# A decoder layer with a spiking delta-rule recurrence: sign weights made earlier, norm roots spread by transposes, two steps of the vector engine's round reordered

## The reference

```python
# 1: a gated delta-rule recurrence, 8 heads, key width 64, value width 128, 512 steps
h = silu(causal_conv4(rms(layernorm(x)) * w_norm_in))
q, k, v = h@wq, h@wk, h@wv              # q and k divided by their norms
step:  mem = 0.9*mem + sd;  hard = mem > 0.5;  mem -= 0.5*spike
       alpha = sigmoid(ab + alpha_spike*spike);  beta = sigmoid(bb + sum(spike*beta_spike))
       s = s*alpha;  s = s - beta*k (k.s) + beta*k v;  out = s.q
y = z + (rms(out)*w_hn) @ w_out * gate(z);  y = y + silu(h2@w_ff1)*(h2@w_ff3) @ w_ff2
x = x + y
# 2: cross attention to 77 context rows, 16 heads, then a layernorm
x = x + layernorm(attention(layernorm(x), ctx) @ Wo + bo + residual)
# 3: three dense layers whose weights are +1 or -1, from boolean arrays
h = [l, -l], l = layernorm(x)
x = x + s2*(2*relu(s1*(2*relu(s0*(h @ sign(k0))) @ sign(k1))) @ sign(k2))
```

## Time and profile before

| | us |
|---|---|
| median of 3 runs | 1086.62 (1082.25 to 1088.74) |
| the profiled execution: its time | 1083.42 |
| its span | 1081.7 |
| PE busy | 964.8 (89%) |
| DVE busy | 680.3 (63%) |
| ACT busy | 503.6 (47%) |
| POOL busy | 208.5 (19%) |

### The profile page before, as it was taken

How to read it: one execution, slowest core, us unless ns; L and a number is a source line. 1 busy time by engine, 2 the same in 40 slices (tenths; PEclk the granted TensorE clock), 3 DMA queues, 4 the chain that set the end, 5 groups by cost and what they waited for, 6 DMA issues and landing times. The chain is left out here.

```text
span 1081.7 us, 40059 instructions
## 1 busy us (share of the span) xinstructions
PE 964.8 (89%) x16722; PEld 643.0 (59%) x16722; DVE 680.3 (63%) x2386; ACT 503.6 (47%) x1506; POOL 208.5 (19%) x394
## 2 busy tenths in 40 slices
PE   7888768999999998999999888889899999999997
PEld 2332246777777777777777776556446446446542
DVE  2887887888888888888767664236335424624710
ACT  7677313555555565555565554413224323423411
POOL 7100200212212122122121220221201210310300
PEclk9999958999999999999999998979999999999999
DMA  3000000000000000000001004000000000000100
GB/s 98 0 1 1 1 2 3 4 4 5 4 5 4 4 5 4 4 5 4 4 4 30 4 5 127 12 10 22 2 1 27 18 1 19 24 1 4 31 0 10
DMA packets 18652, 13.83 MB, mean 13 GB/s; under 512 B 2491, under 2 KB 17259, under 8 KB 18475
## 3 DMA queue, kind: packets, MB, share of 16 engines
q1 hardware_dynamic: 18475, 11.28, 3.7%
HBM read 7.70 MB, written 1.05 MB: 8 GB/s over the span
## 5 line engine op out<-in xcount | busy, mean ns | idle before, releaser
L1087 PE MATMUL banks<-work 64*64 64x64 f32 x3072 | 98.7, 234 | 16.0 <-DVE gates L775 5.9
L1148 PE MATMUL banks<-work 64*64 64x32 f32 x2560 | 106.7, 223 | 6.5 <-ACT work L1550 5.2
L203 DVE SCALAR_TENSOR_TENSOR mom<-gates 128x16 f32<-128x16 f32 x512 | 104.1, 203 | 8.8
L1480 ACT COPY work<-banks 128x128 f32<-128x128 f32 x160 | 43.0, 269 | 136.9 <-PE banks L1123 136.6
L199 DVE SCALAR_TENSOR_TENSOR gates<-mom,gates 128x16 f32<-128x16 f32 x512 | 98.0, 191 | 9.5 <-ACT gates L1453 4.5
L1148 PEld LDWEIGHTS banks<-work 64*64 64x64 f32 x2560 | 91.4, 137 | 18.7 <-issue 10.5
L775 DVE COPY_PREDICATED gates<-work,banks 128x256 f32<-128x256 uint32 x192 | 101.7, 529 | 1.1
L780 DVE TENSOR_TENSOR work<-work,banks 128x128 f32<-128x128 f32 x160 | 45.9, 287 | 83.8 <-PE banks L1148 81.8
L1087 PEld LDWEIGHTS banks<-work 64*64 64x64 f32 x3072 | 73.3, 138 | 34.0 <-issue 23.4
L669 POOL TENSOR_TENSOR mom<-mom 128x4 f32<-128x4 f32 x32 | 6.6, 207 | 387.5 <-ACT work L1529 387.5
L746 DVE TENSOR_TENSOR work<-work 128x256 f32<-128x256 f32 x160 | 68.0, 425 | 17.3 <-PE banks L1087 13.8
(11 more groups left out here) (276 smaller groups left out, 2155.3 us busy)
## 6 DMA issues: line engine op xcount, KB each, us to landing
work<-gates SPq DMA_DIRECT2D x28, 38.5 KB
qT<-in_x_dram SPq DMA_DIRECT2D x4, 256.0 KB, 3.8
work<-in_x_dram SPq DMA_DIRECT2D x4, 256.0 KB, 2.7
out_dram<-work SPq DMA_DIRECT2D x4, 256.0 KB, 2.3
gates<-in_w_ff_dram SPq DMA_DIRECT2D x3, 256.0 KB, 3.1
wv_sb<-in_wv_dram SPq DMA_DIRECT2D x1, 512.0 KB, 5.0
work<-in_w_out_dram SPq DMA_DIRECT2D x1, 512.0 KB, 4.1
gates<-in_x_Wq_dram SPq DMA_DIRECT2D x1, 512.0 KB, 5.3
```

Of the source, the lines that this page charges most:

```text
L203: ve.scalar_tensor_tensor(neg_mem, mem[:, :, t], 1.0, mem[:, :, t], ALU.is_gt, ALU.subtract)\
L1087: last = pe.matmul(level_out(l)[to, a], KS[rows, n.two, hp], late[rows, hp], start=True, stop=True)
L1148: last = pe.matmul(packed(psXT, l)[rows, a], Z[rows, l - 1, z], second_half(XT[:, n.two], l)[rows, a], start=True, stop=True)
L1480: ac.copy(first_half(Z[:, l - 1], l), z_out(l)).then_inc(z_ok, 1)
```

## The change

1. POOL makes the sign weights in the recurrence's pass i = 30 (`prev.it == ROUNDS - 3`), between `root(29)` and `root(30)`, and not at the tail's start; the two small scalings (L1718, L1719) go behind the tail's first root.
2. `spread_root` uses a PE transpose of the broadcast roots where it used a matmul with the identity. The result is the same.
3. PE's `turn_out(prev)` goes from the end of step 3 to step 4, behind `make_z(nxt, 4)`.
4. DVE, step 4: two scan operations stand together ahead of `prefix`, where one was ahead of it and one between `prefix` and `suffix`. Step 5: `prefix`, `suffix` and `keep` follow each other, and four scan operations come behind `keep`, where two of them stood between and one ahead. Steps 1 to 3 are as before.

```diff
                 def body(prev, cur, nxt, aft, aft2, gate, gate_old, scan, ramp):
                     if prev:
                         root(prev)
+                    if prev and prev.it == ROUNDS - 3:
+                        sign_weights()      # the five lines that the tail's start loses, with their waits
                     if aft2:
                         keys(aft2)
...
                         if l == 4 and gate:
                             drive(gate)
-                        spike(scan, h + (4 if l == 4 else 2))
+                        if l < 4:
+                            spike(scan, h + 2)
+                        if l == 4:
+                            spike(scan, h + 4)
+                            spike(scan, h + 5)
                         if aft:
                             prefix(aft, l)
-                        spike(scan, h + (5 if l == 4 else 3))
+                        if l < 4:
+                            spike(scan, h + 3)
                         if aft:
                             suffix(aft, l)
-                        if l != 4:
+                        if l < 4:
                             spike(scan, h + 4)
                         if aft:
                             keep(aft, l)
-                        if l != 4:
+                        if l < 4:
                             spike(scan, h + 5)
+                        if l == 5:
+                            for k in range(2, 6):
+                                spike(scan, h + k)
...
                         if nxt:
                             make_z(nxt, l)
+                        if l == 4 and prev:
+                            turn_out(prev)
...
                         if l == 3 and cur:
                             correct(cur)
-                        if l == 3 and prev:
-                            turn_out(prev)
...
-                gp.wait_ge(tw, TW_SIGN)
-                gp.tensor_scalar(w0_sb, k0_sb, 2.0, -1.0, ALU.mult, ALU.add).then_inc(signs, 1)
-                gp.tensor_scalar(w1_sb, k1_sb, 2.0, -1.0, ALU.mult, ALU.add).then_inc(signs, 1)
-                gp.tensor_scalar(w2_sb, k2_sb, 2.0, -1.0, ALU.mult, ALU.add).then_inc(signs, 1)
-                gp.wait_ge(signs, 3)
-                gp.tensor_tensor(w0_sb[:, 0], w0_sb[:, 0], w0_sb[:, 1], ALU.subtract).then_inc(signs, 1)
-                gp.tensor_scalar(s0x2, v("s0"), 2.0, None, ALU.mult).then_inc(signs, 1)
-                gp.tensor_scalar(s1x2, v("s1"), 2.0, None, ALU.mult).then_inc(signs, 1)
...
                     root(b, 0)
+                    if b == 0:
+                        gp.tensor_scalar(s0x2, v("s0"), 2.0, None, ALU.mult).then_inc(signs, 1)
+                        gp.tensor_scalar(s1x2, v("s1"), 2.0, None, ALU.mult).then_inc(signs, 1)
                     root(b, 1)
...
-                        last = pe.matmul(bank[3][:, n * P:(n + 1) * P], stat[:, 1, n:n + 1].broadcast_to([P, P]),
-                                         ident[:, :], start=True, stop=True)
+                        last = pe.transpose(bank[3][:, n * P:(n + 1) * P], stat[:, 1, n:n + 1].broadcast_to([P, P]),
+                                            ident[:, :])
```

More of the change, by code:

```diff
@@ L671, in root, with sign_weights @@
                     gp.tensor_tensor(ms[:, 1, :], ms[:, 0, :], ms[:, 2, :], ALU.pow).then_inc(rr_ok, 1)
+                def sign_weights():
+                    gp.wait_ge(tw, TW_SIGN)
+                    gp.tensor_scalar(w0_sb, k0_sb, 2.0, -1.0, ALU.mult, ALU.add).then_inc(signs, 1)
+                    gp.tensor_scalar(w1_sb, k1_sb, 2.0, -1.0, ALU.mult, ALU.add).then_inc(signs, 1)
+                    gp.tensor_scalar(w2_sb, k2_sb, 2.0, -1.0, ALU.mult, ALU.add).then_inc(signs, 1)
+                    gp.wait_ge(signs, 3)
+                    gp.tensor_tensor(w0_sb[:, 0], w0_sb[:, 0], w0_sb[:, 1], ALU.subtract).then_inc(signs, 1)
                 def body(prev, cur, nxt, aft, aft2, gate, gate_old, scan, ramp):
```

## The result

The kernel with the change takes 1068.93 us (4 runs, 1068.3 to 1070.37), the kernel before 1087.38 beside it (4 runs): a ratio of 0.984, 95% interval 0.980 to 0.988. A second set of runs on another chip gave 1065.83 against 1085.85, 0.982 (0.979 to 0.985). The forecast was 1067, the range 1060 to 1078. A ratio compares the two kernels over all their runs and is not quite the ratio of the two medians: by the ratios the gain is 17.3 and 19.4 us, by the medians 18.5 and 20.0.

The account below looks back on a forecast made before the run. TensorE, busy for 89% of the span, was taken as the bound: time comes from what it waits for or need not do. Terms 5.5 + 5.9 + 5.0 + 3.5 = 19.9 us off 1086.62 gave 1066.7, forecast 1067, range 1060 to 1078.

Parts of the forecast that it names:

- sign weights and first spread: Tail's start: sign weights and scalings off the first root's path, first spread as a transpose; 5.5 us faster, bounds 2.7 to 6.3.
- fifteen other spreads: Tail's later root spreads as transposes: four k=3 spreads at 0.5 us, eleven at 0.35; 5.9 us faster in all.
- `turn_out` behind `make_z`: Step 4: `make_z` fits into the wait for `normalise`, 0.2 to 0.26 us in 25 of 31 passes; 5.0 us, bounds 0 to 6.5.
- scan operations: Steps 4 and 5 on VectorE: earlier `keep` releases L1082, 0.15 us in each of 24 passes; 3.5 us, bounds -7 to +7.
- the +0.2 us of the clock: Tail's start: net gain taken for when TensorE's clock rises, between 1.0 us gained and 2.6 lost.
- 0.35 each at eleven spreads: Tail spreads other than k=3: each gives 0.31 to 0.50 us, as both paths count; 0.35 taken.
- half of the 0.29 is kept: Pass's end: L1082 comes 0.29 us earlier, `update` 0.3 later; half the gain, 0.15 us a pass, survives.
- The round's end takes it back: Rival: VectorE's later `update` swallows the scan gain and the earlier `turn_out`; 1075, or 1077 with -2 from the recurrence; chance 0.18.
- Scan operations that meet GpSimd: Rival: four scan operations behind step 5's `keep` slow beside GpSimd, 4 x 0.44 us a pass; 1112 us; chance 0.03.
- The clock takes it back: Rival: with transposes for matmuls TensorE's clock falls more often, 1.7 us a fall, and rises late; 1075 us; chance 0.10.
- L1243's wait: Check on TensorE: its wait for ScalarE ahead of L1243 would be gone or below 0.1.
- Passes 1 to 20 shorter by about 0.4 us: Check in the recurrence: the prediction is wrong if these passes do not each get shorter by about 0.4 us.

Follow-up runs that it names:

- after: The kernel with all four parts of the change, against the kernel before: 1068.93 us against 1087.38, ratio 0.984.
- beside part 4: Parts 1, 2 and 4 without part 3 (`turn_out` back at the end of step 3), compared with all four parts: 1073.34 us, ratio 0.989 to the kernel before.
- the scan operations one at a time: All four parts, but the six scan operations behind step 5's `keep` laid singly between the works of the pass's end: 1063.34 us, ratio 0.980 to the kernel before.
- `turn_out` alone: Only part 3, `turn_out` behind `make_z` in step 4, on the kernel before: 1078.95 us, ratio 0.994.
- the spreads alone: Only part 2, the norm roots spread by transposes, on the kernel before: 1076.95 us, ratio 0.993.
- all parts again: The kernel with all four parts once more, on another chip, against the kernel before: 1065.83 us, ratio 0.982.
- sign weights alone: Only part 1, sign weights in pass 30 and two scalings behind the first root, on the kernel before: 1079.68 us, ratio 0.996.

## Why the prediction was right, and where it was not

| term | predicted | measured |
|---|---|---|
| sign weights and first spread | 5.5 | L1812 5.4 sooner in after; 4.7 (1.7 to 7.6) for the move alone |
| fifteen other spreads | 5.9 | 7.4 (15 x 0.49) |
| `turn_out` behind `make_z` | 5.0 | 6.5 (4.0 to 8.9) alone, 7.1 beside part 4 |
| scan operations | 3.5 | -1.2 (-3.5 to +1.0) alone, -0.9 beside the rest |
| sum | 19.9 | 17.3 and 19.4 by the ratios, 18.5 and 20.0 by the medians |

The four parts alone give 17.7 us by the ratios (4.7 + 7.7 + 6.5 - 1.2), and together 17.3 and 19.4: they stand side by side. Part 2's 7.7 (4.7 to 10.9) holds the first spread too. The intervals are too wide to tell 5.0 from 6.5 or 5.9 from 7.4 by time; that these two terms were too small is read from the traces.

**Sign weights, first root.** As worked out: GpSimd off the chain, the spread behind `turn_queries(0)`, GpSimd 3.5 us to spare in pass 30 where 3.8 was expected. For the +0.2 us of the clock no run shows a fixed value: L1822's first 1.0 us ran at half speed in after and 0.2 in its second profile, where L1812's first 1.9 did before.

**The spreads.** The mechanism is right, the term was mis-sized: 0.35 each at eleven spreads. The full difference of 0.49, start to end of one spread, counts at all four of a sequence. So the longer of the two paths decided there; that TensorE, having put its own work behind the spread, soon waits for the norm is the likely reason, but it was not tested by itself.

**`turn_out`.** The fit into the wait is right, and `keep_res` is late next, as named. The term was mis-sized because it priced one wait and the move shortened two: z's copy goes ahead of `turn_out` too, and so `make_x` waits less. The part between the `add_xt` of step 3 and that of step 4 went from 4.02 us to 3.67, 0.35 in a pass (the other kernels without the move have 3.94 to 3.97), where 0.26 was the most that the working allowed.

**The scan operations: the step that failed** is "half of the 0.29 is kept". It failed twice. Its two figures were off, the first by the prediction's own count of operations: the chain behind `keep` grew from two dependent operations to five, 3 x 0.22 = 0.67, less the 0.20 by which `keep` comes earlier, so `update` is 0.49 later and not 0.3; and L1082 comes 0.19 earlier and not 0.29. But even with `update` put early, nothing is gained. By `make_z` of step 1 0.12 of the 0.19 is left, by `make_xt` 0.05, and the pass is 16.29 us with part 4 against 16.30 without. Part of it is the wait that the prediction named: `level` in step 1 waits 0.2 us for VectorE's last `keep` in 8 of 20 passes (1.6 us, against the 4.3 gained at L1082). But with the scan operations one at a time that wait is gone and the pass is no shorter. What takes the rest was not isolated. At varying places in a pass TensorE is idle behind nothing that the profile names, as here, ahead of `make_z` in after:

```profile
460.24 0.43 PE L1141 MATMUL banks<-work,gates 64*64 64x32 f32 x15 [0.67 <-issue]
```

Such a pause could absorb 0.2 us; that is argued, and stays open. That the sum came out is luck in part: this term's 3.5 us or more too much stood against some 3 us too little in the spreads and `turn_out` (1.5 and 1.5 to 2.1).

**The rivals.** *The round's end takes it back* was right in that the scan order gives nothing, and wrong in that `turn_out` would be swallowed too: 7.1 us beside part 4. *Scan operations that meet GpSimd*: the median of one is 193 and 185 ns (L203, L199) in after and 192 and 183 before, and none of the five behind step 5's `keep` took over 0.20 us in 21 passes; not seen. (Its price of 4 x 0.44 us does not follow from 0.51 against 0.19, which is 0.32.) *The clock takes it back*: not seen. In the tail the half-speed stretch at its start is 6.9 us (1.5 to 8.4), before it was 13.7, and the later fall of 3.4 us is absent in after and there in the second profile of the same kernel; it comes and goes in kernels with and without transposes. The Trainium skill, TensorE: Matmul & The Clock Gate, Part 4, has a PE-mode transpose not count as busy for the gate. By that rule the first spread as a transpose would have made the rise later than as a matmul. The profiles do not show it: 6.3 to 9.1 us with the transposes, 7.2 and 8.3 with the matmul, `turn_queries` matmuls on both sides of it. A scatter of 3 us could hide a small effect, and the rule itself, over a longer stretch, is shown by no run.

**The prediction's own checks.** L1812, the 64 records, 0.65 us a call and the sign weights' place are as said. L1243's wait is 1.2 us over 7 times, not below 0.1 in all. The wait of TensorE in step 1 is there, 1.6 us in 20 passes, but VectorE's is not gone (0.53 at the boundary above). "Passes 1 to 20 shorter by about 0.4 us" is missed in the profile of after, 16.52 us from 16.70, with one stretch of 3.4 us at half clock among them, and met in the other three profiles with all four parts or nearly so (16.24 to 16.29). It stood on `turn_out` and the scan order together and came from `turn_out`, which gives 0.34 alone (16.36).

**Versions as good.** Parts 1 to 3 without part 4, and with the scan operations one at a time, are each about 2% under the kernel before and can't be told from the kernel after. Part 4 may as well be left out.

## What to carry to other kernels

Short work whose input is long there belongs into a wait for another engine, and its price is read by what it releases as well as by the wait that it fills: here it filled one wait and shortened a second. A piece of work that comes earlier is worth only what the next wait behind it lets through; before pricing it at half, look for the next thing that its engine waits for. Count the dependent operations on either side of what is moved, at 0.22 us each here, and not only the ones moved.

## What the runs showed of the chip that was not expected

The stretch up to the first `update` is the prologue and the passes i = -3 to 0, in which only the scan order differs between these kernels. Yet the first `update` starts at 189.0 to 196.9 us, and early or late roughly as TensorE had been at half clock ahead of it (from windows over 100 us to the first `update`; all have another 6.8 to 13.6 us at half clock before that):

| kernel | half clock in that stretch, us | first update, us |
|---|---|---|
| `turn_out` alone | 34.1 | 189.0 |
| before | 34.1 | 189.4 |
| the spreads alone | 47.8 | 193.3 |
| all parts again | 41.0 | 194.7 |
| after | 47.8 | 195.6 |
| sign weights alone | 51.2 | 196.9 |

The same kernel, after, stands in it twice with different values, and `turn_out` and the sign weights touch nothing there. This is most of why the spans of before and after differ by 13.0 us and the medians by 18.5. In the two profiles that stretch is 6.2 us longer in after, the 28 passes from the first `update` on are 5.6 shorter (459.6 to 454.0), and the tail is 14.8 shorter (382.2 to 367.4); 1.2 us go the other way between the passes and the tail. The passes scatter too: with `turn_out` moved, those 28 took 445.6 to 454.0 us in seven profiles of kernels with the scan, without it 456.6 to 459.6 in five. A profile's whole span can't price a part of a few us; a stretch that begins and ends at instructions near the change can.
